# One copy and two gate products moved in the V stage of a gated-delta-rule attention kernel

## The reference, cut to what matters

```python
xn = _layernorm(x)
q = silu(short_conv(xn @ Wq)); k = silu(short_conv(xn @ Wk)); v = silu(short_conv(xn @ Wv))
beta = sigmoid(xn @ Wb); g = -exp(A_log) * softplus(xn @ Wa + dt_bias)
# per head, per token: S = S * exp(g); S += k (beta (v - k S)); o = q S     (q and k normalised)
o = gated_delta_rule(q, k, v, g, beta)            # 6 heads, 64 wide keys, 128 wide values
gate = xn @ Wg                                    # 2048 x 768
o = o * rsqrt(mean(o * o) + eps) * norm_weight * silu(gate)
x + o @ Wo + feed_forward(xn)                     # the weights of the second branch are splines
```

## Time and profile before

| | us |
|---|---|
| timed runs | 869.08, 876.75, 876.76 |
| median | 876.75 |
| the profiled execution's own time | 871.43 |
| its span in the trace | 869.9 |
| mean granted clock of PE, share of full speed | 0.953 |
| busy: PE, DVE, ScalarE, POOL | 775.7, 574.6, 471.1, 384.8 |

### The profile page before, as it was taken

The page is one execution under the profiler, slowest core; times in us unless marked ns, Lnnn a source line. Parts: engine busy times, 40 slices in busy tenths (PEclk is TensorE's granted clock), DMA queues, the critical chain, the costliest instruction groups (busy, mean ns, idle before and its releaser), DMA issues.

```text
span 869.9 us, 15485 instructions
## 1 busy us (share of the span) xinstructions
PE 775.7 (89%) x5688; PEld 451.5 (52%) x5688; DVE 574.6 (66%) x1400; ACT 471.1 (54%) x1078; POOL 384.8 (44%) x419
## 2 busy tenths in 40 slices
PE   2989379998978999987999997899579999999998
PEld 1455157656547756645774655665124444444443
DVE  4889957768876778894877896568554544444400
ACT  3757746654875764685665486668553333333300
POOL 2376977567792655586355667022341000000000
PEclk9989789998989999898999899999799999999999
DMA  6502021330021031003023001054855222222011
GB/s 201 201 14 48 5 75 40 101 78 19 17 78 46 30 111 61 1 0 119 11 98 88 11 1 34 6 172 124 229 121 170 73 73 73 73 61 72 25 61 36
DMA packets 59936, 62.20 MB, mean 72 GB/s; under 512 B 30391, under 2 KB 45100, under 8 KB 59862
## 3 DMA queue, kind: packets, MB, share of 16 engines
q1 hardware_dynamic: 53526, 44.97, 18.3%
q0 software_dynamic: 4224, 13.11, 4.9%
q10 hardware_dynamic: 2112, 3.15, 1.1%
HBM read 33.69 MB, written 19.73 MB: 61 GB/s over the span
## 4 chain that ended last, share of the span: by engine, by line
PE 60%; DVE 14%; POOL 10%; issue 6%; SPq 5%; DMA 3%; ACT 2%; POOLq 0%; ACTq 0%; DVEq 0%
PE bank L643 14%; PE pd L1983 6%; PE pd L1984 6%; PE pd L1985 6%; SPq L423 5%; PE bank L729 3%; DVE cv L1040 2%; PE bank L803 2%; PE bank L720 2%; POOL cv L1627 2%; PE bank L855 2%; POOL rn L1608 1%; PE pg L1969 1%; PE bank L831 1%; DVE BA L1210 1%
## 5 line engine op out<-in xcount | busy, mean ns | idle before, releaser
L643 PE MATMUL bank<-x_parts,w 128*128 128x512 f16 x576 | 130.2, 384 | 1.5 <-DVE x_parts L997 1.5
L2055 DVE TENSOR_TENSOR hh<-sg,pu 128x512 f32<-128x512 f32 x64 | 43.9, 687 | 103.0 <-ACT sg L2022 90.7
L643 PEld LDWEIGHTS bank<-x_parts,w 128*128 128x128 f16 x576 | 56.2, 99 | 69.7 <-issue 6.9
L1927 POOL DMA_DIRECT2D yr<-y_attn x16 | 8.8, 553 | 185.2 <-DMA out<-yr 185.2
L643 PE MATMUL bank<-w,x_parts 128*128 128x384 f16 x384 | 77.1, 359 | 7.9 <-ACT V L1404 7.7
L2022 ACT ACTIVATE sg<-pg 128x512 f32<-128x512 f32 x64 | 38.0, 594 | 71.6 <-PE pg L1970 71.3
L643 PEld LDWEIGHTS bank<-w,x_parts 128*128 128x128 f16 x384 | 39.3, 107 | 39.0 <-issue 9.9
L1608 POOL TENSOR_TENSOR rn<-t,mhalf 128x6 f32<-128x6 f32 x16 | 22.8, 1424 | 73.6 <-DVE t L1203 73.6
L1040 DVE SCALAR_TENSOR_TENSOR cv<-raw,taps,cv 128x512 f32<-128x512 f32 x72 | 53.5, 808 | 0.0
L1983 PE MATMUL pd<-dw,it 128*128 128x512 f16 x128 | 48.8, 381 | 0.0
L1984 PE MATMUL pd<-dw,it 128*128 128x512 f16 x128 | 48.8, 381 | 0.0
(11 more groups left out here) (310 smaller groups left out, 2053.1 us busy)
## 6 DMA issues: line engine op xcount, KB each, us to landing
xb<-in_x SPq DMA_DIRECT2D x4, 1024.0 KB
xr<-in_x SPq DMA_DIRECT2D x16, 256.0 KB, 2.6
y_attn<-xr SPq DMA_DIRECT2D x16, 256.0 KB
down_rows<-inv SPq DMA_DIRECT2D x8, 512.0 KB, 5.8
yr<-y_attn POOLq DMA_DIRECT2D x16, 256.0 KB, 2.9
out<-yr SPq DMA_DIRECT2D x16, 256.0 KB, 2.0
xn_hi<-x_parts POOLq DMA_DIRECT2D x4, 512.0 KB
xn_lo<-x_parts POOLq DMA_DIRECT2D x4, 512.0 KB
```

The lines of the kernel that those rows point to most:

```text
L643: ins = nc.tensor.matmul(out, a, b, start=first and i == 0, stop=last and i == 2)
L2055: v.tensor_tensor(hh[:, i % 2, :], sg[:, i % 2, :], pu[i % 2][:], ALU.mult).then_inc(h_ready, 1)
```

## The change

Two things are moved, and nothing is added or taken away.

- On PE the gate products (1,0) and (1,1) leave their places behind blocks 6 and 7 and stand behind V transpose 1, ahead of the solve. The ring of banks is changed to fit: blocks 6 to 11, V transposes 0 and 1, gates (1,0), (1,1) and (2,0), V transpose 2. From V transpose 2 on each entry has the bank that it had.
- On ScalarE the two silus of these gates stand behind V block 1, ahead of `place_inverses`. V block 0 is copied ahead of silu 10, where it stood behind it. The Silu table is loaded where the first silu of the V stage stands, which was gate silu (1,0) and is now silu 6.

```diff
@@ bank_uses
-    for n in range(NV):
-        ring += [("blk", NQK + n)] + (gates[2 + n:3 + n] if n < 2 else [])
-    ring += [("vtr", 0), ("vtr", 1), gates[4], ("vtr", 2), ("vtr", 3), gates[5], ("vtr", 4), ("vtr", 5)] + gates[6:]
+    ring += [("blk", NQK + n) for n in range(NV)]
+    ring += [("vtr", 0), ("vtr", 1), gates[2], gates[3], gates[4], ("vtr", 2), ("vtr", 3), gates[5], ("vtr", 4), ("vtr", 5)] + gates[6:]
@@ local, PE
                     block_products(s, NQK + n)
                     if n == 0:
                         query_sums(s)
-                    if n < 2:
-                        gate_products(s, 1, n)
                 v_transposes(s, 0)
                 if before is not None:
                     ready(pe, ("KQ", NCH - 1, LATE_BANK - 4), s)
                     project_out(before, NCH - 1)
                 v_transposes(s, 1)
+                for h in range(2):
+                    gate_products(s, 1, h)
                 solve(s)
@@ local, ScalarE
                 for n in range(NV):
                     v_taps(s, NQK + n)
-                    if n < 2:
-                        gates(s, 1, n)
                     if n < NV - 1:
                         raw_out(s, NQK + n + 1)
+                    if n == NV - 1:
+                        v_tokens(s, 0)
                     if n >= 1:
                         silu(s, NQK + n - 1)
-                v_tokens(s, 0)
                 v_tokens(s, 1)
+                for h in range(2):
+                    gates(s, 1, h)
                 place_inverses(s)
                 silu(s, NBLK - 1)
```

## The result

The changed kernel takes 880.93 us (median of 4 runs, 878.98 to 885.37) against 872.91 us before (median of 4 runs, 866.39 to 876.76). The ratio is 1.0133, with a 95% interval of 1.0086 to 1.018: **slower by 1.3%**, where the forecast was 875.8 us and no change that a measurement would show. The ratio is not the quotient of the two medians, which is 1.0092. The profiled executions stand at 881.16 and 871.43 us.

What follows compares the result with a forecast made beforehand. PE was taken as the bound, busy 775.7 of 869.9 us, with the V chain through POOL and ScalarE delaying the solve. 3 x 1.05 - 0.9 = +2.25 us on 873.5 gave 875.8 us, range 868 to 883.

Steps and rivals of the forecast that it cites:

- Term 1: V stage, super-tiles after the first: without gate (1,0) in its way, the V chain runs 2.23 us earlier.
- Rival (b): V stage: ScalarE makes POOL wait at blocks 8 and 9, so the V chain gets no shorter; 882.4 us, chance 0.12.
- Term 2: End of V stage on ScalarE: V block 0 copied ahead of silu 10 frees its bank for PE 3.35 us earlier.
- Term 3: PE before the solve: two more gates and X(0) cost 4.4 us, making V transpose 2 and X(1) 1.05 us later.
- Rival (c): PE before the solve: the moved gates turn out free, as in the first super-tile; 862.6 us, chance 0.04.
- Term 5: ScalarE: moved silus and table load before silu 6 are covered, adding nothing; at most 3.8 us if the load's cover fails.
- Term 4: PE's wait before the solve: the clock falls as before, its loss moving from gate (2,0) to gate (1,0); net nothing.
- Term 6: First super-tile: gates fit in PE's 12.90 us wait for DVE's inverse; gate (2,0) may find the clock up, -0.9 us.
- DVE stays as it is: DVE: its work is unaffected, its copy of X(0) being hidden behind gate (2,0) in the new order; nothing added.
- The rivals: Clock stays up, 869.7 us (chance 0.17); V chain not shorter, 882.4 us (0.12); gates free, 862.6 us (0.04).

Runs made afterwards that it cites:

- the filler: Twelve matmuls (ten in e12) with unread results, added on PE in its wait behind V transpose 1; on the changed kernel with the hold, ratio 0.9986.
- e13: Kernel before, with the filler on PE between V transpose 1 and X(0); ratio 0.9985.
- e9: Changed kernel, with POOL held in the first super-tile and twelve unread matmuls on PE ahead of gate (1,0); ratio 0.9986.
- c_after_again: The changed kernel itself, timed again as a control against the kernel before; ratio 1.0113.
- the hold: In the first super-tile only, POOL waits after its first tap sum until DVE's 21 spline steps are done; on the changed kernel, ratios 1.0136 and 1.0072.
- e4: Kernel before, with two extra POOL sums, results unused, in the first super-tile while POOL waits for block 7; ratio 1.0063.
- e3: Changed kernel, with POOL held in the first super-tile until DVE's spline steps are done; ratio 1.0136.
- e3b: Changed kernel with the hold on POOL in the first super-tile, timed again on another chip; ratio 1.0072.
- e5: Kernel before, with gates (1,0) and (1,1) moved behind blocks 8 and 9 and V block 0 copied ahead of silu 10; no hold; ratio 1.002.
- e6: Kernel before, with gates (1,0) and (1,1) behind blocks 8 and 9, V block 0 ahead of silu 10, and the hold; ratio 0.9991.
- e7: Kernel before, with gates (1,0) and (1,1) behind blocks 7 and 8 and V block 0 ahead of silu 10; no hold; ratio 0.9943.
- e8: Kernel before, with gates (1,0) and (1,1) behind blocks 7 and 8, V block 0 ahead of silu 10, and the hold; ratio 0.9934.
- e11: Changed kernel, with the filler on PE ahead of gate (1,0) and without the hold; ratio 1.003.
- e1: Kernel before, with only V block 0's copy moved ahead of silu 10, gates in their old places; ratio 1.0002.
- e12: Kernel before, with gates behind blocks 7 and 8, V block 0 ahead of silu 10, the hold, and ten filler matmuls ahead of X(0); ratio 0.9949.
- e2: Changed kernel, with V block 0 copied behind silu 10 as before, so only the gates are moved; ratio 1.0175.
- e10: Kernel before, with only the hold on POOL in the first super-tile added; ratio 0.9985.

## Why the prediction was wrong, point by point

- **Term 1, the V chain starts earlier (2.23 us): right.** 2.29 us by block 11's taps, 2.26 by block 8's halo, and POOL shows no wait for ScalarE. Rival (b) is out.
- **Term 2, the bank free 3.35 us earlier: right**, 3.57. (The term's own figures, 252.97 less 249.52, give 3.45.)
- **Term 3, +1.05 us per super-tile: right once the clock is equal.** With the filler in both orders, X(1) stands at +31.44 in the old one (e13) and +32.40 in the new one (e9), both in the second super-tile, and +31.43 and +32.39 in the third: +0.96. In the profiled pair it was -0.07, -1.72 and +0.92. Rival (c), the gates free, is out.
- **Term 5, the table load covered: right.** The silu starts 0.01 us after the load, and raw 9 (242.62 + 0.57) was there before POOL's halo at 243.58. The drain that the Trainium skill adds (ScalarE: Activation LUTs, What ACT_TABLE_LOAD costs), by which the sum would have been 3 us higher, does not show in the trace: between the copy ahead of the load and the silu behind it ScalarE is idle for 0.03 us beside the load's 1.28.
- **Term 4, the clock nets to nothing: wrong in its reach.** The fall did move from gate (2,0) to gate (1,0), and the Trainium skill describes such falls (TensorE: Matmul & The Clock Gate, HAM oscillation — how this bites in real kernels): waits between bursts of matmuls let the clock fall, and each burst then begins slow. The gates behind the wait, 5.39 us without the filler and 4.07 with it, agree. What was not foreseen is that the move changes what follows: the clock comes back early, and falls again in the solve's tail: from X(1) to the first norm scale the three super-tiles take 1.31, 1.58 and 1.58 us longer than before. Up to X(1) the profiled pair shows no loss, because the kernel before has falls of its own (its X(1) at +33.76 and +35.43 against +31.44 and +31.43 with the filler). So it is luck that the three super-tiles' +3.6 us lie near the 3 x 1.05 = 3.15 of the sum: the forecast had them ahead of X(1), and they came behind it.
- **How much of the loss is the clock's: 3 to 6 us, and not settled.** In the timed runs the filler is worth 0.86% in the new order and 0.15% in the old. The difference, 0.7% or 6 us, is one measure; with the intervals of the three ratios taken together (the root of the sum of their squared half-widths, 0.55%) it is just told from nothing. The mean clocks of the timed runs give another, an estimate: among the executions of the kernel before, in each of the four batches, the time is 5.7 to 7.2 us shorter for each 0.01 of clock, and the changed kernel's clock was 0.0052 lower (c_after_again), which makes 3 to 4 us. By the same estimate the 0.0047 more clock that the filler gave the old order should bring 0.3 to 0.4%; 0.15% was measured, within its interval.
- **Term 6 and "DVE stays as it is": the step that failed, by the profiles the largest miss.** The forecast gave the first super-tile -0.9 us; it cost +6.2 up to the next one, 4.7 of it ahead of X(0). These 7.1 us are all that the profiled pair's 9.3 has over the forecast sum of +2.25. Gate (2,0) behind it did not find the clock up either (4.02 us, before 3.64). "Nothing is added", said the term; its argument took the 12.90 us wait for DVE's inverse as a fixed cover, under which the gates and an earlier V chain are free. DVE's end was not fixed: POOL's sums, moved 2.2 us forward, fell on DVE's spline steps. The hold removes this in every profile (spline 6.8 to 6.9), e4 makes it in the old order. Timed, the hold is worth less than the 4.7 us of the profile: the five pairs without and with it differ by -0.03% (after and e3), 0.41% (c and e3b), 0.29% (e5 and e6), 0.09% (e7 and e8) and 0.44% (e11 and e9), with intervals that overlap in each; weighted by these intervals, 0.3% with some 0.2% either way, about 2.5 us.
- **Do the parts close?** Hold and filler together take 1.0113 to 1.0133 down to 0.9986, the level of the old order with either (0.9985), so no large third cause is left. The +0.96 us per super-tile of term 3, 0.3% in all, is inside the intervals of that comparison. How the loss divides among collision, clock and term 3 is not known to better than 2 to 3 us.
- **The rivals.** None of the three was what happened, and none had the end of DVE's work in it. The loss came near the time given to (b), 882.4 us, by other causes; the range held it, by luck, and slower by over 1% had been given a chance of 0.10. The trace of before had the warning: the first super-tile was the one place where DVE set the end, what else ran beside DVE there was not looked at, and the step at 76.70 already took 1.35 us beside a tap sum instead of 0.29.
- **Open.** Stretches of some 13.6 us at half clock appear in the tail of one super-tile in six profiles (e1, e3b, e6, e8, e9, e11), whatever the order of the gates; no run tells what brings them. Each puts some 5 us on its super-tile (31.1 to 31.9 us from X(1) to the first norm scale instead of 25.8 to 26.5), as much as the effects that are looked for here, so a single profile doesn't tell what an order is worth. Of the timed executions only the mean clock is known, not where it fell.

## What to carry to other kernels

A wait that is long enough to hide work is a cover only if its end stays where it is: when a chain on another engine is moved, look at what it will now run beside, on the engine that ends the wait above all. Before work is moved behind a wait of PE's, count the clock for the whole stage that follows, not for the next product alone. Here the same early start of the V chain, with the gate products one block later instead of behind the wait, made a kernel 0.5 to 0.7% faster than the one before (e7, e8 and e12).

## What the runs showed of the hardware

- **A short DVE step that meets a POOL sum lasts until the sum ends.** A 128x128 step that reads SBUF alone took 0.29 us, and 1.2 to 1.4 us when a 128x512 tap sum of 1.27 us was under way on POOL; the copy (1.18 us for 0.23) and the scaling at L478 (1.45 for 0.43) did the same. The inverse's steps, one of whose inputs or whose output is in PSUM, did not: 0.21 us at 91.88 beside POOL's sum at 91.39. The Trainium skill has this rule (SBUF — State Buffer, Who interferes with whom): DVE with two inputs in SBUF, or in a two-port form of a copy or scaling, shares a lock with GpSimd that is held for a whole instruction. The trace agrees, and adds the price for a chain of short steps: nearly one POOL instruction for each.
- **The collision's size is a matter of a microsecond or two between two chains.** Three profiles with the same gate positions and no hold gave 11.12, 15.89 and 12.9 us for the same 21 steps. In all profiles without the hold and without added sums the size follows the time at which ScalarE copies block 7 in the first super-tile, on which POOL's further sums wait, while DVE begins its steps at 73.6 to 74.0 in each: with the copy at 76.2 (c, e5) ten steps are lengthened and the total is 15.9 us; at 77.4 and 77.8 (e11, e2) seven, 12.9; at 78.4 (after) five, 11.1; at 78.7 (e7) four, 9.7; from 79.8 on (e1, before, e13) one, 6.8 to 6.9. The old order is not safe by its order alone: in the profile of e10 its block 7 was copied at 78.1, and there the hold was in place.
- **The clock fell where PE was busy.** In 278.50 to 282.20 PE worked all 3.70 us and was granted 0.54, behind 20 us at 1.00 in which it had worked 17.41; with the filler in the wait ahead of the gates (e9, second super-tile), the same work ran at 1.00 to its end, but in the third it met a long stretch at half clock; in the kernel before it ran at 1.00 although the gate behind the wait had run slow, and in e12 it did not although the gates had all run fast. So a change of work some 20 us earlier moves such a fall, and no simple rule of these runs says where to.
